# Attention maxima split and turned one slot later on DVE, placed one slot later on POOL

## The reference

```python
def _lora_linear(x, W, A, B):
    return x @ W + SCALING * (x @ A @ B)
q = _lora_linear(hidden_states, Wq, Aq, Bq).reshape(bsz, q_len, NH, HD)
k = _lora_linear(traces, Wk, Ak, Bk).reshape(bsz, t_len, NKV, HD)
v = _lora_linear(traces, Wv, Av, Bv).reshape(bsz, t_len, NKV, HD)
...
scores = jnp.einsum('bhqd,bhtd->bhqt', q, k) / jnp.sqrt(jnp.asarray(HD, q.dtype))
attn = jax.nn.softmax(scores, axis=-1)
context = jnp.einsum('bhqt,bhtd->bhqd', attn, v)
out = _lora_linear(context, Wo, Ao, Bo)
return hidden_states + out
```

## Time and profile before

| | us |
|---|---|
| median of 3 runs | 685.08 (685.04 to 685.62) |
| profiled execution | 685.43 |
| its span | 683.2 |
| PE busy | 666.6 (98%) |
| DVE busy | 518.6 (76%) |
| ACT busy | 468.5 (69%) |
| POOL busy | 368.4 (54%) |

### The profile page before, as it was taken

One profiled execution on the slowest core, in us unless ns is written; L12 is line 12 of the kernel. 1 busy time (PEld: TensorE's weight loads), 2 busy tenths in 40 slices (PEclk: granted clock), 3 DMA queues, 4 the chain that ended last, 5 costly groups with the idle time before them and its releaser, 6 DMA issues.

```text
span 683.2 us, 14789 instructions
## 1 busy us (share of the span) xinstructions
PE 666.6 (98%) x4220; PEld 527.1 (77%) x4220; DVE 518.6 (76%) x1173; ACT 468.5 (69%) x1462; POOL 368.4 (54%) x316
## 2 busy tenths in 40 slices
PE   8999999999999999999999999999899999999998
PEld 6797777877877787787788778777676788888886
DVE  4768888787787778778777877878887898855542
ACT  5657888888888888888888888887678443222220
POOL 3548634852772484376258437625867005876732
PEclk9999999999999999999999999999999999999999
DMA  8957665674676567466656756657567244655331
GB/s 275 342 178 194 199 191 157 198 205 133 178 209 190 161 194 208 154 172 191 184 163 195 205 172 169 189 185 215 183 209 226 90 138 155 215 185 185 123 119 66
DMA packets 103797, 124.67 MB, mean 182 GB/s; under 512 B 9280, under 2 KB 85312, under 8 KB 103760
## 3 DMA queue, kind: packets, MB, share of 16 engines
q1 hardware_dynamic: 103760, 124.23, 59.9%
HBM read 86.18 MB, written 38.01 MB: 182 GB/s over the span
## 4 chain that ended last, share of the span: by engine, by line
PE 62%; DVE 20%; ACT 9%; issue 6%; DMA 2%; DVEq 0%; ACTq 0%; POOL 0%; SPq 0%; POOLq 0%
PE banks L1665 17%; PE banks L1472 12%; DVE neg_max L1128 7%; PE banks L1490 7%; PE banks L1531 6%; PE banks L1470 6%; PE banks L1520 5%; ACT banks L897 5%; PE banks L1507 5%; DVE turned_sb L1149 4%; PE banks L1451 2%; DVE x_both L1169 2%; ACT probs_t L908 2%; DVE q_stage L1120 2%; DVE max_parts L1137 1%
## 5 line engine op out<-in xcount | busy, mean ns | idle before, releaser
L897 ACT ACTIVATE banks<-banks,neg_max 128x256 f32<-128x256 f32 x512 | 230.3, 453 | 37.5 <-DVE neg_max L1128 32.9
L781 POOL TENSOR_TENSOR q_stack<-turned_sb,head_mask 8x512 fp32r<-8x512 f32 x128 | 138.6, 1083 | 189.2 <-DVE turned_sb L1149 183.0
L1128 DVE TENSOR_REDUCE neg_max<-banks 128x2 f32<-128x512 f32 x256 | 174.8, 686 | 34.3 <-PE banks L1490 32.1
L908 ACT ACTIVATE probs_t<-banks 128x512 f32<-128x512 f32 x256 | 155.1, 606 | 47.2 <-PE banks L1507 46.5
L1472 PE MATMUL banks<-x_both,w_hi 128*128 128x512 f32 x448 | 162.5, 395 | 0.0
L1470 PE MATMUL banks<-x_both,w_lo 128*128 128x256 f32 x448 | 118.4, 280 | 0.0
L1490 PE MATMUL banks<-k_stack,q_stack 96*128 96x256 f32 x512 | 113.7, 304 | 4.2 <-ACT banks L897 3.4
L1490 PEld LDWEIGHTS banks<-k_stack,q_stack 96*128 96x128 f32 x512 | 79.8, 190 | 45.2 <-issue 20.2
L897 ACT ACTIVATION_READ_ACCUMULATOR banks<-banks,neg_max 128x1 f32 x512 | 107.4, 210 | 0.0
L1507 PE MATMUL banks<-q_stack,k_stack 104*128 104x512 f32 x256 | 102.0, 399 | 0.0
L1470 PEld LDWEIGHTS banks<-x_both,w_lo 128*128 128x128 f32 x448 | 84.6, 189 | 9.2
(11 more groups left out here) (156 smaller groups left out, 1150.1 us busy)
## 6 DMA issues: line engine op xcount, KB each, us to landing
q_stack<-q_parts SPq DMA_DIRECT2D x192, 128.0 KB, 3.0
q_parts<-q_stage SPq DMA_DIRECT2D x64, 256.0 KB, 3.7
raw<-ct SPq DMA_DIRECT2D x32, 256.0 KB, 3.8
raw<-xt SPq DMA_DIRECT2D x32, 256.0 KB, 3.9
scales<-r_rows SPq DMA_DIRECT2D x64, 128.0 KB
context<-ctx_stage SPq DMA_DIRECT2D x64, 128.0 KB, 3.8
stage<-xn SPq DMA_DIRECT2D x16, 512.0 KB, 5.1
w_hi<-context SPq DMA_DIRECT2D x14, 512.0 KB, 6.9
```

The source lines that it names most:

```text
L781: nc.gpsimd.tensor_tensor(q_stack[rows, u % RING, heads], turned_sb[rows, u % 2].unsqueeze(1).broadcast_to([M_ROWS, 2, S]), head_mask[rows ...
L897: last = nc.scalar.activation(score_bank[c % 2][:, S * h:S * (h + 1)], score_bank[c % 2][:, S * h:S * (h + 1)], ACT.Exp, bias=neg_max[:, u ...
L908: nc.scalar.activation(probs_t[:, u % 2, t, 2 * hp:2 * hp + 2, :].rearrange("p a b -> p (a b)"), st_bank[j % 2], ACT.Exp, scale=-1.0).then ...
L1128: nc.vector.tensor_reduce(out=neg_max[:, u % 2, 2 * c:2 * c + 2], in_=score_bank[c % 2].rearrange("p (h t) -> p h t", h=2), axis=AXIS, op= ...
```

## The change

Two places change. DVE's `split_max` and `turn_max` of group `u` stand in the slot with `c == 1` instead of `c == 0`, so `row_max` of the first scores of group `u+1` comes before them. `TURN` goes from 1 to 2, so POOL's `place_max` stands in the slot with `c == 2`.

```diff
-TURN = 1
+TURN = 2
...
-                if c == 0 and here:
+                if c == 1 and here:
                     split_max(b, u)
-                if c == 0 and u >= 0 and not (last and u > NG):
+                if c == 1 and u >= 0 and not (last and u > NG):
                     turn_max(b, u)
```

## The result

| | before | after |
|---|---|---|
| median, us | 685.06 (4 runs) | 716.75 (4 runs, 715.02 to 719.08) |
| ratio | | 1.046, 95% interval 1.045 to 1.047 |
| profiled execution, us | 685.43 | 717.54 |
| its span, us | 683.2 | 715.4 |

The change makes the kernel slower by 31.7 us. It was forecast slower, at 705.3 with a range of 694 to 718; the measured time is near the range's upper end, so the forecast loss of 20 us was about 12 us short. One of the four runs (719.08) lies outside the range.

The account below looks back on a forecast made before the run. PE was taken as the bound for most of the span. Six loop batches at +2.6 us, batch 0 at +4.6 and the last at 0 gave +20.2 on the profiled 685.43, or 705.3 us against the median; range 694 to 718.

Parts of the forecast that it names:

- the four groups named: Slots 9, 17, 25, 33: a late second row maximum makes PE stand 0.65 us in each, 2.6 a batch.
- the 1.0 us between slots 16 and 24: Time lost per loop batch before the change, all of it counted as gained: -1.0 a batch.
- batch 0: First batch: the loop's costs plus low-rank pieces, less the 3.3 us lost now: +4.6.
- low-rank pieces: Seven in batch 0's slots with c == 1, ahead of the second row maximum, 0.70 us each: 4.3 net.
- the blocked operation: Casts in slots 9 and 17 held up by POOL: 0.5 and 0.3 us, 0.8 a batch.
- the stack of group 0: Next batch's load behind SP's later store, with no cover left: 0.2 us a batch, bounds 0 and 0.5.
- the last batch: Folds freed from behind the turn against late fourth scores: gain and loss set equal, 0, bounds -3 and +5.
- No cost: POOL's later placing still has the transposed scores' heads ready when PE wants them; 1.6 us in a group if a split late.
- Faster: Rival: the late second row maximum costs nothing and only the gains stay, 674.7 us; chance 0.08.
- no difference: Rival: stalls and gains cancel, 0.25 us a group instead of 0.65, 685 us; chance 0.07.
- SP did not become the bound: Rival judged: the later turn fully delays group 0's stack, PE waits 2.0 us more each batch, 718 us; chance 0.10.
- The casts blocked in full: Rival: the shared port blocks casts for whole POOL instructions, 2.6 for 0.8 us a batch, 718 us; chance 0.10.

Follow-up runs that it names:

- The last batch as before: Changed kernel, but with split, turn and placing of the last batch left where they were before the change: 712.70 us, ratio 1.039.
- group 5 alone: Kernel before, with split, turn and placing one slot later for group 5 only, in batches 0 to 6: 682.02 us, ratio 0.995.
- the folds first: Changed kernel, with the fold's total and high part ahead of split and turn in the last batch's slots with c == 1: 719.48 us, ratio 1.050.

## Why the prediction was right, and short

**Right.** The bound, the loop through two score banks, and its place. In each loop batch exactly the four groups named are long and the other four are at PE's own 7.30; the 1.0 us between slots 16 and 24 shows no more as such; the first row maximum is at C + 1.55, SP's store at C + 3.74. The plain case, slots 24 and 32, is 0.74 for 0.65: the fourth scores are 0.64 late, and 0.1 more passes because behind a wait the context stands 1.72 behind the fourth scores (325.99 to 327.71), not 1.62 (308.36 to 309.98).

**Right in part by luck: batch 0.** With what is ahead of it, it was forecast +4.6 and is +4.3, but two errors meet in it. The low-rank pieces were all priced by the row of L1060, 0.70 us; the three in slots 5, 9 and 13 are casts (L1052), from whose start to the next operation only 0.21 passes, and the groups of slots 8 and 12 are as in the loop (9.16 and 7.28), without the 0.70 and 0.55 forecast for their pieces. The four pieces of L1060 hold: 0.54 to 0.62 each over the loop's groups, forecast 0.55 and 0.70. Against that, the subtract is blocked here too, in slot 9 (1.23 us) and already in slot 5 (0.89 us), ahead of the first context.

**The term that was mis-sized in the loop: the blocked operation.** The prediction had 0.5 in slot 9 and 0.3 in slot 17, and blamed the cast. Measured: 1.11 in slot 9 (1.28 less 0.17), near the bound of 1.29, and it was the subtract; in slot 17 the cast lost 0.24 (0.41 for 0.17), and x parts blocked ahead of it (1.39 and 0.92 us for 0.69) delayed the row maximum of scores 20 to C + 1.71, 0.17 more. With four times 0.1 behind the waits, and the 0.2 for the stack of group 0 that did not come, 2.6 becomes 3.5 a batch. Moving POOL's split away gave exactly the 1.1 back in that group. I should have run the rows on: POOL's second half began at 303.81 already, and the prediction itself has POOL later. And the row that I took as measure, 0.23 lost, was an accident of where POOL stood; the same trace has a cast that was blocked nearly in full, in batch 0, DVE and then POOL:

```profile
62.25 1.16 DVE L1137 CAST max_parts<-neg_max 128x8 fp32r<-128x8 f32 x1
...
62.10 1.29 POOL L773 TENSOR_TENSOR c_both<-raw,c_both 128x512 fp32r<-128x512 f32 x1
```

Here the cast ends 0.02 us behind POOL's instruction, in the row of 302.22 it was 0.03. The price is what is left of that instruction, not a share of it.

**The term that was missed: the last batch.** Forecast 0 with bounds -3 and +5, measured +6.6, outside these bounds. The working had the fourth scores late by C + 6.7 but set against it a gain for PE of the same size without adding the two up group by group. The trace shows two things that eat that gain. The projection of slot 7 (11, 15) may only start once the fold's high part of slot 5 (9, 13) is through, and that stands behind the turn too (three waits of up to 1.4 us, L1451); all listed waits of PE in the last batch together rose from 6.4 to 8.8 us. And behind such waits the granted clock fell, in 480 to 545 us of the span to a mean of 0.92, where it was 0.97 before: three stretches of some 3 us at the lower level (1.2 GHz), where it was one. If PE did only half its work in them, the two more cost up to some 3 us, an estimate from these rows. The last batch as before brought 4.1 us back. How much of that is the clock and how much the waits was not separated. The runs of the change spread over 4 us (715.0 to 719.1), and go with their granted clock (0.999, 0.995, 0.993, 0.990 from the fastest to the slowest); that the clock is the cause of the spread was not tested. It isn't the cause of the loss: the fastest run, at 0.999, is still 30.0 us above the kernel before.

**POOL.** "No cost" was right as to waits: nobody waited for the placing. Alone it costs 0.65 a batch all the same, by blocking x parts; the prediction priced POOL by its due dates only, not by what runs beside it on DVE.

**The rivals.** Faster and no difference are out: the terms hold to 0.1. SP did not become the bound through the turn; the load of group 0 kept pace. One wait of 0.99 us for a DMA came in batch 1 (163.08, group 7's stack, whose slowest load took 5.7 us to land, where it was 4.9 at the same place in batch 4); the same wait, 0.9 to 1.1 us, stands in the profiles of four of the kernels built on the change, and its cause stayed open. The casts blocked in full, 718, came nearest, with the right mechanism (an operation held up by POOL's whole instruction) in one of its two places. That the median fell inside the range owes something to luck: the upper end, 718, was set by the two slower rivals (SP, the casts), while the loss in excess of the forecast came from the blocked subtract (0.6 a batch), several terms of 0.1 to 0.2, and the last batch.

## What to carry to other kernels

An operation that is moved past one other is paid for by whoever stands behind it: write down the start of each instruction that gates a shared buffer, before and after, from measured distances, and compare with its due date. A slot that holds the long foreign work (here the context block) is the place for long work of one's own; one that is moved on should go only where the next slot is empty, as group 5 alone showed (682.0 against 685.3). Where DVE and POOL both work on tiles in SBUF, look at what runs beside the moved operation, not only at who waits for whom.

## What the runs showed of the hardware

- A 128x8 subtract on DVE, both inputs in SBUF, took 1.28 us beside a POOL instruction of 1.29 us, and 0.17 elsewhere. In the twelve traces, 208 of the casts and subtracts of `max_parts` began with over 0.17 us of a POOL tensor_tensor still to run. They took 0.21 to 1.30 us, and every one ended 0.02 to 0.03 us behind POOL's instruction. The 1195 with no POOL instruction beside them took 0.16 or 0.17.
- The 128x512 subtract (L1169) took 0.68 us alone. The 179 that began with over 0.2 us of a POOL tensor_tensor still to run all ended 0.54 to 0.55 us behind it (0.76 to 1.77 us long): they did most of their work when it was through. For the small operations the block is many times their own length.
- The granted clock fell from 1.00 to 0.50 in the last batch, for some 3 us each time, behind waits of 0.6 to 1.7 us: once in the kernel before, three times in the change, four times with the folds first (means 0.97, 0.92 and 0.89 over the same 65 us). PE's listed waits in the last batch were 6.4, 8.8 and 10.7 us. Not every such wait was followed by a fall: none came behind those of 1.36 and 0.61 us at 506.1 and 507.7 us of the changed kernel.
